# A graph network in one launch: the first layer's weights product as float16 halves, three small operations moved to GpSimd, the product placed five matmuls later

## The reference, cut to what matters

```
h = max(layernorm(x), 0)
for layer in (1, 2):
    norm = 1 / sqrt(max(deg_out[src], 1) * max(deg_in[dst], 1))
    msg  = (h[src] @ W1 + (h[src] * h[dst]) @ W2) * norm
    agg  = sum of msg over the edges of each dst
    h    = h @ W1 + agg
    h    = max(h, 0)            # layer 1 only
out = x + h
```

## Time and profile before

| | |
|---|---|
| median of three executions | 559.8 us |
| profiled execution, its own time | 558.2 us |
| its span, first to last instruction | 556.5 us |
| before layer 1 | 0 to about 225 us |
| layer 1, from its first matmul | about 225 to 395.6 us |
| layer 2 | 395.6 to about 552 us |
| one position of layer 1 | 3.38 us |
| one position of layer 2 | 3.13 us |

### The profile page before, as it was taken

The page is one execution under the profiler, slowest core; times in us unless marked ns, Lnnn a source line. Parts: engine busy times, 40 slices in busy tenths (PEclk is TensorE's granted clock), DMA queues, the critical chain, the costliest instruction groups (busy, mean ns, idle before and its releaser), DMA issues.

```text
span 556.5 us, 19281 instructions
## 1 busy us (share of the span) xinstructions
PE 497.2 (89%) x7774; PEld 456.0 (82%) x7774; DVE 428.5 (77%) x1162; ACT 252.8 (45%) x709; POOL 179.8 (32%) x328
## 2 busy tenths in 40 slices
PE   0299578898988996799999999999999999999995
PEld 0177467776877886699999999999899999999995
DVE  4689399999797999877777777777766666666673
ACT  0278478898988996333333333333211111111111
POOL 3659968787899999000000000000000000000000
PEclk9999799998999999699999999999999999999999
DMA  2113900000000000000000000000000020002011
GB/s 69 53 38 84 176 6 17 8 15 7 17 7 16 9 15 1 1 3 3 2 2 4 1 3 2 4 1 3 2 2 2 2 41 2 2 4 39 1 26 18
DMA packets 19429, 9.88 MB, mean 18 GB/s; under 512 B 16081, under 2 KB 18657, under 8 KB 19342
## 3 DMA queue, kind: packets, MB, share of 16 engines
q1 hardware_dynamic: 18222, 5.93, 5.8%
q0 software_dynamic: 1120, 2.72, 1.9%
HBM read 5.19 MB, written 1.65 MB: 12 GB/s over the span
## 4 chain that ended last, share of the span: by engine, by line
PE 35%; DVE 27%; issue 14%; POOL 12%; ACT 8%; DMA 2%; DVEq 0%; SPq 0%; POOLq 0%; ACTq 0%
PE diff L798 25%; DVE mixed L585 7%; DVE los L549 5%; PE slab L740 4%; POOL h L447 3%; POOL hist L400 2%; PE diff L725 2%; ACT h L879 2%; DVE work L672 2%; PE diff L782 2%; DVE work L650 2%; POOL words L403 2%; DVE work L656 2%; DVE work L659 2%; DVE rdi_sc L663 1%
## 5 line engine op out<-in xcount | busy, mean ns | idle before, releaser
L798 PE MATMUL diff<-los,mixed 128*128 128x129 f16 x2401 | 159.4, 222 | 7.9 <-DVE los L629 7.3
L549 DVE TENSOR_TENSOR los<-mixed,iota_bank 128x6144 bf16<-128x6144 bf16 x49 | 161.4, 3339 | 0.2 <-PE slab L740 0.2
L798 PEld LDWEIGHTS diff<-los,mixed 128*128 128x128 fp8e4 x2401 | 153.3, 101 | 10.0 <-issue 7.4
L798 PE MATMUL diff<-late,mixed 128*128 128x128 f16 x2401 | 150.7, 219 | 1.1 <-DVE late L675 1.1
L798 PEld LDWEIGHTS diff<-late,mixed 128*128 128x128 fp8e4 x2401 | 145.6, 98 | 2.0 <-DVE late L675 0.7
L740 PEld LDWEIGHTS slab<-hots,los 128*128 128x128 bf16 x2352 | 122.1, 100 | 24.7 <-ACT saved L840 10.1
L740 PE MATMUL slab<-hots,los 128*128 128x98 fp8e5 x2352 | 129.1, 211 | 7.1 <-DVE los L549 6.8
L832 ACT ACTIVATE hots<-diff 128x784 f16<-128x784 f32 x147 | 118.3, 846 | 9.1 <-PE diff L725 8.9
L585 DVE TENSOR_SCALAR mixed<-words 128x400 int32<-128x400 int32 x294 | 91.7, 367 | 0.0
L725 PE MATMUL diff<-select,mixed 80*128 80x392 f16 x294 | 69.9, 344 | 19.5 <-ACT hots L832 12.6
L403 POOL TENSOR_SCALAR words<-saved 128x392 uint16<-128x392 uint16 x98 | 85.8, 875 | 0.4
(11 more groups left out here) (125 smaller groups left out, 368.6 us busy)
## 6 DMA issues: line engine op xcount, KB each, us to landing
mixed<-rows SPq DMA_DIRECT2D x147, 12.0 KB, 1.8
x_sb<-in_x_dram SPq DMA_DIRECT2D x4, 384.0 KB
out_dram<-x_sb SPq DMA_DIRECT2D x8, 128.0 KB
los<-in_dst_dram SPq DMA_DIRECT2D x1, 750.0 KB
out_dram<-x_sb SPq DMA_DIRECT2D x4, 80.0 KB
out_dram<-x_sb SPq DMA_DIRECT2D x4, 48.0 KB
los<-samples,row_i POOLq DMA_INDIRECT x7, 2.6
wt<-in_L_gnn_W_dram SPq DMA_DIRECT2D x4, 16.0 KB, 2.1
```

What stands on the lines that cost most here:

```text
L549: nc.vector.tensor_tensor(out=los[:, b % LOS_RING].rearrange("e s (v t) -> e s v t", t=2), in0=key, in1=val, op=ALU.is_equal).then_inc(los ...
L798: ins = nc.tensor.matmul(acc[a][:, 0:width], tiles[:, a, q], parts[:, q, 0:width], start=(q == 0), stop=(q == BLOCKS - 1))
```

## The change

It does the following.

1. The weights product of layer 1 is made of float16 halves: `second_scale` gets three operations that scale the first layer's weights by `scale1` and split them in two halves (`w0_parts`). ScalarE saves the turned pair as its float16 high half, VectorE subtracts for the low half (`low_turned`, 128 x 128 from PSUM), and `weigh` issues four float16 matmuls of 64 columns in place of a float32 one. In layer 2 it stays float32.
2. `low_turned(n)` stands in VectorE's queue between the second and the third of the four unpacking operations of position n.
3. GpSimd takes three pieces of work: `product` (`pair[1]`, 128 x 64, in both layers), `factors` (two operations of 128 x 1: `rdi * rdo` and the scale for h) and `low_part` (the low half of g1, 128 x 64), in this order in layer 1; at position 49 `low_part(48)` comes ahead of `product(49)`. TensorE waits for `product_ready` before the transpose.
4. ScalarE clips the old h of n+1 (`keep_positive`) after the reads of the sums of n, no longer ahead of them. Its new h waits for the scale of GpSimd and for the pair.
5. `LATE` goes from 40 to 45.
6. `rdo_sc1` (line 639) goes; `rdi_sc1` is replaced by `rdi_rdo`.

The diff, cut to its core:

```diff
-LATE = 40
+LATE = 45
...
+            def product(n):
+                b, a = n % BLOCKS, n % 2
+                pool.wait_ge(s_ready, n + 1)
+                if n >= 2:
+                    pool.wait_ge(t_ready, n - 1)
+                if n < BLOCKS:
+                    pool.wait_ge(h_ready, n + 1)
+                else:
+                    pool.wait_ge(z_used, min(n - BLOCKS + 1, BLOCKS))
+                nc.gpsimd.tensor_tensor(out=pair[a][:, 1], in0=s_sum[a], in1=h[:, b], op=ALU.mult).then_inc(product_ready, 1)
+
+            def factors(b):
+                pool.wait_ge(rdi_ready, b + 1)
+                nc.gpsimd.tensor_tensor(out=rdi_rdo[:, b:b + 1], in0=rdi[:, b:b + 1], in1=rdo[:, b:b + 1],
+                                        op=ALU.mult).then_inc(g_scale, 1)
+                nc.gpsimd.tensor_scalar(rdi_h[:, b:b + 1], rdi[:, b:b + 1], unscale1[:, 0:1], UNIT, ALU.mult,
+                                        ALU.mult).then_inc(h_scale, 1)
+
+            def low_part(b):
+                pool.wait_ge(hi1_ready, b + 1)
+                nc.gpsimd.tensor_tensor(out=parts1[:, b, D:2 * D], in0=g1[b % 2], in1=parts1[:, b, 0:D],
+                                        op=ALU.subtract).then_inc(parts1_ready, 1)
+
+            pool.wait_ge(rdo_kept, 1)
+            for n in range(POSITIONS):
+                if n == BLOCKS:
+                    low_part(n - 1)
+                product(n)
+                if n < BLOCKS:
+                    factors(n)
+                if 0 < n < BLOCKS:
+                    low_part(n - 1)
...
+                v(nc.vector.tensor_scalar(w0_scaled, wt[:, 0], scale1[:, 0:1], None, ALU.mult))
+                v(nc.vector.tensor_copy(w0_parts[:, 0], w0_scaled))
+                v(nc.vector.tensor_tensor(out=w0_parts[:, 1], in0=w0_scaled, in1=w0_parts[:, 0], op=ALU.subtract))
...
+                    dve.wait_ge(product_ready, n - 1)
                 nc.vector.scalar_tensor_tensor(s_sum[a], acc[a][:, D:2 * D], unscale, s_hi[a],
                                                ALU.mult, ALU.add).then_inc(s_ready, 1)
                 if n < BLOCKS:
                     nc.vector.tensor_scalar(root[:, b:b + 1], root_in[:, b:b + 1], 1.0, None,
                                             ALU.max).then_inc(clip_ready, 1)
+                    dve.wait_ge(clip_ready, n + 1)
                 dve.wait_ge(s_ready, n + 1)
-                nc.vector.tensor_tensor(out=pair[a][:, 1], in0=s_sum[a], in1=h[:, b], op=ALU.mult)
...
-                    v(nc.vector.reciprocal(rdi[:, b:b + 1], root[:, b:b + 1]))
-                    v(nc.vector.tensor_tensor(out=rdi_sc1[:, b:b + 1], in0=rdi[:, b:b + 1], in1=rdo_sc1[:, b:b + 1],
-                                              op=ALU.mult))
+                    nc.vector.reciprocal(rdi[:, b:b + 1], root[:, b:b + 1]).then_inc(rdi_ready, 1)
+
+            def low_turned(n):
+                a = n % 2
+                dve.wait_ge(t_hi_saved, n + 1)
+                nc.vector.tensor_tensor(out=halves_t[a][:, 1], in0=t_ps[a][:, 0:128], in1=halves_t[a][:, 0],
+                                        op=ALU.subtract).then_inc(t_lo_saved, 1)
...
+                    dve.wait_ge(g_scale, n + 1)
                     if n >= 2:
-                        dve.wait_ge(hi1_ready, n - 1)
-                    nc.vector.tensor_scalar(g1[a], turn_z[a][:, 0:D], rdi_sc1[:, b:b + 1], 0.0,
+                        dve.wait_ge(parts1_ready, n - 1)
+                    nc.vector.tensor_scalar(g1[a], turn_z[a][:, 0:D], rdi_rdo[:, b:b + 1], 0.0,
                                             ALU.mult, ALU.max).then_inc(g1_ready, 1)
-                    dve.wait_ge(hi1_ready, n + 1)
-                    nc.vector.tensor_tensor(out=parts1[:, b, D:2 * D], in0=g1[a], in1=parts1[:, b, 0:D],
-                                            op=ALU.subtract).then_inc(parts1_ready, 1)
...
-                        unpack(n + 2)
+                        unpack(n + 2, (0, 1))
+                    if n < BLOCKS:
+                        low_turned(n)
+                    if n + 2 < POSITIONS:
+                        unpack(n + 2, (2, 3))
...
+                pe.wait_ge(product_ready, n + 1)
...
+                if n < BLOCKS:
+                    for half in range(2):
+                        for part in range(2):
+                            ins = nc.tensor.matmul(turn_z[a][:, 0:D], halves_t[a][:, half], w0_parts[:, part],
+                                                   start=(half + part == 0), stop=(half + part == 2))
+                    ins.then_inc(z_ready, 1)
+                else:
+                    nc.tensor.matmul(turn_z[a][:, 0:D], pair_t[a], wt[:, 1], start=True, stop=True).then_inc(z_ready, 1)
...
+                if n < BLOCKS:
+                    nc.scalar.activation(halves_t[n % 2][:, 0], t_ps[n % 2][:, 0:128], ACT.Copy).then_inc(t_hi_saved, 1)
+                else:
+                    nc.scalar.activation(pair_t[n % 2], t_ps[n % 2][:, 0:128], ACT.Copy).then_inc(t_saved, 1)
...
+                        act.wait_ge(h_scale, n)
+                        act.wait_ge(pair_ready, n)
+                        act.wait_ge(product_ready, n)
...
-                        act.wait_ge(normed, n + 1)
-                        nc.scalar.activation(h[:, b], h[:, b], ACT.Relu).then_inc(h_ready, 1)
...
+                    if n + 1 < BLOCKS:
+                        keep_positive(n + 1)
```

More of the change, by code:

```diff
@@ L171, in fast_path @@
     rdi = sb("rdi", [128, BLOCKS], FP32)
-    rdi_sc1 = sb("rdi_sc1", [128, BLOCKS], FP32)
+    rdi_rdo = sb("rdi_rdo", [128, BLOCKS], FP32)
     totals = sb("totals", [128, 2], FP32)
@@ L208, in fast_path @@
     pair = [work_f[:, (6 + 2 * i) * D:(8 + 2 * i) * D].rearrange("p (k f) -> p k f", k=2) for i in range(2)]
+    halves_t = [work[:, (10 + 2 * i) * D:(12 + 2 * i) * D].bitcast(FP16).rearrange("p (k f) -> p k f", k=2) for i in range(2)]
+    rdi_h = spread[:, 0]
+    w0_scaled = words_late[:, 1024:1024 + D]
     pair_t = [work_f[:, (10 + 2 * i) * D:(12 + 2 * i) * D] for i in range(2)]
@@ L267, in fast_path @@
     deg_rooted = sem("deg_rooted")
+    rdo_kept = sem("rdo_kept")
     scaled_ready = sem("scaled_ready")
@@ L278, in fast_path @@
     t_ready = sem("t_ready")
+    t_hi_saved = sem("t_hi_saved")
+    t_lo_saved = sem("t_lo_saved")
     t_saved = sem("t_saved")
+    rdi_ready = sem("rdi_ready")
+    g_scale = sem("g_scale")
+    h_scale = sem("h_scale")
+    product_ready = sem("product_ready")
     z_ready = sem("z_ready")
@@ L573, in second_scale, with unpack @@
                 v(nc.vector.tensor_scalar(unscale1[:], power[:], 2.0 ** -14 / UNIT, None, ALU.mult))
-            def unpack(n):
+                v(nc.vector.tensor_scalar(w0_scaled, wt[:, 0], scale1[:, 0:1], None, ALU.mult))
+                v(nc.vector.tensor_copy(w0_parts[:, 0], w0_scaled))
+                v(nc.vector.tensor_tensor(out=w0_parts[:, 1], in0=w0_scaled, in1=w0_parts[:, 0], op=ALU.subtract))
+            def unpack(n, fields=range(4)):
                 if n >= 2:
@@ L579, in unpack @@
                     "p (q w) -> p q w", w=WORDS // 2)
-                for s in range(4):
+                for s in fields:
                     to = tile_words[:, n % 2, :, 8 * s:8 * s + 8]
@@ L586, in unpack @@
                                                       ALU.bitwise_and)
-                ins.then_inc(tile_ready, 1)
+                if 3 in fields:
+                    ins.then_inc(tile_ready, 1)
             find_begin(0, 1)
@@ L616, in _ @@
             dve.wait_ge(deg_rooted, 1)
-            v(nc.vector.reciprocal(rdo[:], rdo[:]))
+            nc.vector.reciprocal(rdo[:], rdo[:]).then_inc(rdo_kept, 1)
+            dve.wait_ge(rdo_kept, 1)
             v(nc.vector.tensor_scalar(rdo_sc0[:], rdo[:], SC0, None, ALU.mult))
@@ L638, in _ @@
             dve.wait_ge(words_copied, UNITS)
-            nc.vector.tensor_scalar(rdo_sc1[:], rdo[:], scale1[:, 0:1], None, ALU.mult)
             def sums(n):
@@ L767, in turn_pair @@
                 pe.wait_ge(pair_ready, n + 1)
+                pe.wait_ge(product_ready, n + 1)
                 if n >= 2:
-                    pe.wait_ge(t_saved, n - 1)
+                    pe.wait_ge(t_hi_saved, min(n - 1, BLOCKS))
+                    pe.wait_ge(t_lo_saved, min(n - 1, BLOCKS))
+                if n - 2 >= BLOCKS:
+                    pe.wait_ge(t_saved, n - 1 - BLOCKS)
                 nc.tensor.transpose(t_ps[a][:, 0:128], pair[a].rearrange("p k f -> p (k f)"),
@@ L774, in weigh @@
                 a = n % 2
-                pe.wait_ge(t_saved, n + 1)
+                if n < BLOCKS:
+                    pe.wait_ge(t_lo_saved, n + 1)
+                else:
+                    pe.wait_ge(t_saved, n + 1 - BLOCKS)
                 if n >= 2:
@@ L781, in weigh @@
                         pe.wait_ge(z_used, BLOCKS)
-                nc.tensor.matmul(turn_z[a][:, 0:D], pair_t[a], wt[:, n // BLOCKS], start=True,
-                                 stop=True).then_inc(z_ready, 1)
```

(23 more changed lines are left out.)

4 lines of the change are left out of this document (1 added, 3 removed).

## The result

| | before | changed |
|---|---|---|
| median | 559.55 us (4 runs, 558.88 to 560.95) | 568.12 us (4 runs, 565.96 to 568.5) |
| profiled execution | 558.2 us, span 556.5 | 565.96 us, span 564.2 |

The ratio is 1.0149, with a 95% interval of 1.0126 to 1.0171: the change makes the kernel 1.5% slower, as forecast (568.2, range 558 to 577).

What follows compares the result with a forecast made beforehand. Bound: layer 1's loop over three engines, not TensorE alone. Period 0.40+1.09+0.75+1.27 = 3.51 against 3.38: 6.1 us over 47, 0.29 at the first weights product, 2.0 between layers, +8.4 in all; 566.6 profiled, 568.2 median, range 558 to 577.

Steps and rivals of the forecast that it cites:

- The bound is a loop over three engines with EARLY-to-LATE in it: Layer 1: a 2.40 us chain over three engines plus TensorE's 0.98 from transpose to weights product make the 3.38 period.
- ScalarE's clip saves 0.15: Layer 1, ScalarE: clipping after the reads shortens the chain from 672 to 650 from 1.24 to 1.09 us.
- TensorE's floor: Layer 1: TensorE's own work, 3.24 us a position before; as a rival, period 3.20 to 3.24, 554.6 us, chance 0.16.
- The weights product: Layer 1, TensorE: four float16 matmuls gain between nothing and 0.06 us; 0.03 taken, so 0.40 to line 672.
- The meeting of product and pair: Layer 1: GpSimd's product and VectorE's 659 run together; transpose 0.65 to 0.90 us after 650, 0.75 taken.
- the case of the full meeting: 659 waits out GpSimd's product, then takes its full 0.28: transpose at 0.90, period 3.66, 575.3 us; chance 0.08.
- LATE is the dear part: Layer 1, TensorE: five matmuls more between transpose and weights product, 0.98 to 1.27 us, counting in full on the loop.
- VectorE has 0.12 to spare, and GpSimd beside the unpacking costs nothing: Layer 1: VectorE free for 672 at 2.30 us, result at 2.42; nothing charged for GpSimd's 0.6 us.
- That rival: Layer 1: VectorE becomes the bound once GpSimd takes over 0.12 us from it; 571 to 577 us, chance 0.14.
- the ring: Layer 1's loop, 3.38 us a position; VectorE called as tight, 672 starting the moment the last unpacking ends.
- Factors at 0.15 each: GpSimd: two one-column operations at 0.15 us each, 0.30 within the 3.01 wait between the layers.
- `second_scale` at nothing: Three added operations, some 0.6 us, fall into VectorE's idle 8.93 us before the nodes' rows and cost nothing.

Runs made afterwards that it cites:

- the 256 columns: One useless GpSimd operation of two 256-column SBUF inputs added per layer 1 position to the kernel before: 575.19 us in one execution, beside 559.88.

## Why the prediction was right

The direction, the mechanism and the number held, the number closer than its parts: the 47 periods came out 2.1 us below the forecast, and 1.25 us more than forecast ahead of layer 1's first weights product, for which no cause is shown, made up for most of it. That the total met is luck to this extent. By the prediction's own steps:

| step | predicted | measured |
|---|---|---|
| weights product to g1 | 0.40 | 0.32 |
| g1 to `s_sum` | 1.09 | 1.10 |
| `s_sum` to transpose | 0.75 | 0.76 |
| transpose to weights product | 1.27 | 1.27 |
| period | 3.51 | 3.45 |
| 47 periods | +6.1 us | +4.0 us |
| between the layers | +2.0 us | +2.2 us |
| layer 2 | 0 | -0.01 us |
| ahead of the weights product of block 0 | +0.3 us | +1.55 us |
| profiled execution | 566.6 us | 565.96 us |

- *The bound is a loop over three engines with EARLY-to-LATE in it*: shown by LATE = 45 alone (+0.30 a position) and by the clip alone (-0.14), and the clip is worth 0.15 in the changed kernel too.
- *ScalarE's clip saves 0.15*: right (0.14 and 0.15). TensorE's floor, 3.24, was 0.05 too high for a transpose that doesn't wait.
- *The weights product*: the mis-sized term. Even the more favourable bound, a gain of 0.06, was too small: 844 takes 385.81-385.69 = 0.12 of the queue and its result is there 0.32 after its start, 0.11 sooner than before. I had taken 0.03.
- *The meeting of product and pair*: the transpose at 0.76 is the forecast's 0.75. Of the Trainium skill's rule (SBUF — State Buffer, "SBUF: two separate sides") the runs bear out the exclusive lock, by the 256 columns. That the loser then needs its whole length is what the prediction made of it, and did not happen: it needs 0.08, and the case of the full meeting, 0.90, fell.
- *LATE is the dear part*: right, and the result of `low_turned` is ready at 0.97 to 1.02 after the transpose (388.55+0.29-387.87, and a hop), where 1.02 was forecast; LATE = 41 sufficed.
- *VectorE has 0.12 to spare, and GpSimd beside the unpacking costs nothing*: the unpacking stayed at 0.36 a record, the low half's removal left the period at 3.46. VectorE became the bound only with LATE = 41, at 3.29; so it had 0.16 to spare. That rival was near and did not happen. The prediction was wrong, though, that VectorE was as tight as the ring in the kernel before; it had some 0.04 to spare: there 672 starts 0.32 after the last unpacking, where back to back is 0.28, and with LATE = 45 it still comes 0.42 after 782. Merged rows overstated VectorE's part.
- *Factors at 0.15 each*: they took 0.23 and 0.39, one column each, against 0.27 for 49 columns. Those 0.32 more account for the 0.26 by which the stall between the layers, 3.27, exceeded the forecast's 3.01.
- *`second_scale` at nothing*: the three operations took 1.3 us, not 0.6, but VectorE was still idle for 8.51 behind them, so the cover held.
- Four of the 47 periods are longer, by 0.35, 0.11, 0.11 and 0.23, 0.8 us in all. The kernel before and its versions have none. In two the late operation is one of VectorE's (698, 705), in two one of ScalarE's (965, 954). ScalarE's stay at blocks 31 and 44 where ScalarE's program is that of the changed kernel; VectorE's move from 21 and 30 to 11, 28 and 45 in both versions with the low half back on VectorE. With the clip put back, which alters ScalarE's order, block 31 is not late and 44 by only 0.06. So the place depends on the program and not on the data; what the engine waits for there, no trace shows.
- The median is 2.2 us above the profiled execution, and the forecast put 1.6 there by analogy. That it met 568.12 to a tenth is luck.

## What to carry to other kernels

Where engines hand one position round in a ring, add up the links from start to start. What is taken off an engine that is not a link gains nothing. Where the ring passes through two inserts in TensorE's queue, every matmul between them is part of a link, though TensorE looks busy all the time. Try the parts of a change one by one, since here one instruction moved in ScalarE's queue gained 7 us or more and the other parts together cost 15. Here the operation moved to GpSimd also held up VectorE's two-input one, to 0.08 after its own end, and it delayed whatever followed in GpSimd's queue; ask what waits for the last thing in that queue.

## What the runs showed that I had not expected

In two of the four traces with a long idle time between the layers, TensorE's granted clock was halved behind it. In the changed kernel's trace the granted clock stayed at 1.00 behind it and 27 matmuls took 1.70. In the run with the product on VectorE, after an idle time of 2.80 us, the same 27 took 3.04, at a granted clock of 0.50, which is 1.2 GHz:

```profile
400.33 3.04 PE L853 MATMUL diff<-late,mixed 128*128 128x128 f16 x27 [2.80 <-POOL late L500]
```

The same stretch by busy time (TensorE, its weight loads, VectorE, ScalarE, GpSimd, then the granted clock):

```profile
400.33:403.50 3.17, 3.17 (x30) 3.10 (x31) 0.00 (x0) 0.00 (x0) 0.00 (x0) 0.50 0.03 5
```

The run with the clip put back shows it too (3.04 after 2.96 idle), LATE = 41 in the changed kernel doesn't (1.70 after 2.65). No version with the short stall does. From the weights product of block 47 to that of block 48 it is 6.00 us in the changed kernel, 7.57 with the clip put back and 8.32 with the product on VectorE. It may be why the other three executions of the changed kernel were 2 us slower than the profiled one, but this is not shown: they left no trace, and their mean clocks on record, 0.968 to 0.971 beside 0.973, differ no more than those of the kernel before do among themselves (0.967 to 0.976).

GpSimd needs 0.23 and 0.39 us for operations of a single column, about as much as for 64 (0.32), while 256 took 0.65: up to 64 columns, what was moved there is priced by the instruction more than by its size.
